# Key tile first, in four pieces, and maxima among the last projections, in a fused attention and FFN kernel

## What is computed

```python
h = layernorm(x)
q  = rms_norm(h @ wq)
k  = rms_norm(ctx @ wk);   ki = rms_norm(ctx @ wki)   # ki for the first 257 rows, k for the rest
v  = ctx @ wv;             vi = ctx @ wvi
x  = x + (attention(q, k, v) + attention(q, ki, vi)) @ wo
t  = layernorm(layernorm(x))[:, -1] @ agg             # one row of each batch
for _ in range(4):
    t = t + gelu(layernorm(t) @ d1) @ d2
y  = layernorm(x)
x  = x + layernorm(y + sigmoid(y @ wg) * (t @ bc))
```

## Time and profile before

| | us |
|---|---|
| runs (three) | 608.13, 610.99, 612.56 |
| median | 610.99 |
| span of the profiled execution | 607.0 |
| PE busy in it | 533.4 (88%) |
| DVE busy | 392.7 (65%) |
| ACT busy | 282.7 (47%) |
| POOL busy | 240.7 (40%) |

### The profile page before, as it was taken

How to read it: one execution, slowest core, us unless ns; L and a number is a source line. 1 busy time by engine, 2 the same in 40 slices (tenths; PEclk the granted TensorE clock), 3 DMA queues, 4 the chain that set the end, 5 groups by cost and what they waited for, 6 DMA issues and landing times.

```text
span 607.0 us, 9796 instructions
## 1 busy us (share of the span) xinstructions
PE 533.4 (88%) x3768; PEld 325.9 (54%) x3768; DVE 392.7 (65%) x750; ACT 282.7 (47%) x504; POOL 240.7 (40%) x138
## 2 busy tenths in 40 slices
PE   2589799999978999989999988898998998999860
PEld 2478668987644555545555454454444544554320
DVE  5547886433965787558776686476565747368676
ACT  3355744552124566426565253536362443376342
POOL 0032330032024766545655533243333345467453
PEclk9988989999979999979999998899999998799976
DMA  7506667599469699927888571707061713100001
GB/s 284 169 1 242 238 248 278 171 209 313 157 165 317 146 214 239 223 88 171 204 214 214 159 170 71 170 10 163 26 146 71 170 37 109 71 1 35 17 37 52
DMA packets 56327, 91.35 MB, mean 150 GB/s; under 512 B 5316, under 2 KB 30276, under 8 KB 55768
## 3 DMA queue, kind: packets, MB, share of 16 engines
q1 hardware_dynamic: 52032, 74.93, 45.8%
q0 software_dynamic: 3184, 14.16, 7.2%
q10 hardware_dynamic: 1064, 1.63, 1.0%
HBM read 70.84 MB, written 19.40 MB: 149 GB/s over the span
## 4 chain that ended last, share of the span: by engine, by line
PE 70%; DVE 16%; ACT 5%; POOL 3%; issue 2%; DMA 2%; SPq 0%; POOLq 0%; ACTq 0%; DVEq 0%
PE psum L673 14%; PE psum L767 12%; PE psum L730 10%; PE psum L748 10%; PE psum L772 5%; PE psum L802 5%; DVE negt L1154 4%; PE psum L891 3%; PE psum L856 3%; PE psum L837 2%; DMA qst<-crow 1%; DVE negm L1152 1%; DVE attT L1170 1%; POOL ssum L1323 1%; POOL ssum L1321 1%
## 5 line engine op out<-in xcount | busy, mean ns | idle before, releaser
L999 ACT ACTIVATE prob<-psum 128x512 f32<-128x512 f32 x256 | 138.6, 593 | 179.9 <-PE psum L748 175.0
L1154 DVE TENSOR_REDUCE negt<-psum 128x1 f32<-128x255 f32 (+1 forms) x256 | 129.2, 545 | 0.0
L1371 POOL TENSOR_TENSOR added<-added,prob 128x1024 f32<-128x1024 f32 x48 | 114.0, 2375 | 24.4 <-ACT prob L999 19.9
L730 PE MATMUL psum<-kst,qst 96*128 96x512 f32 x256 | 100.3, 468 | 5.3 <-DVE negt L1154 5.2
L1368 POOL TENSOR_TENSOR added<-prob 128x1024 f32<-128x1024 f32 x16 | 39.5, 2466 | 158.7 <-ACT prob L999 158.7
L1152 DVE TENSOR_REDUCE negm<-psum 128x1 f32<-128x257 f32 x128 | 53.6, 418 | 74.2 <-PE psum L730 73.6
L748 PE MATMUL psum<-qst,kst 100*128 100x256 f32 x512 | 94.9, 306 | 4.7 <-DMA qst<-crow 3.4
L767 PE MATMUL psum<-prob,vring 128*32 128x256 f32 x1152 | 94.1, 411 | 1.7 <-issue 0.5
L748 PEld LDWEIGHTS psum<-qst,kst 100*128 100x128 f32 x512 | 81.8, 200 | 24.5 <-ACT prob L999 9.6
L730 PEld LDWEIGHTS psum<-kst,qst 96*128 96x128 f32 x256 | 41.4, 195 | 67.5 <-issue 39.6
L1321 POOL TENSOR_TENSOR ssum<-sq 128x512 f32<-128x512 f32 x6 | 9.5, 1585 | 110.7 <-ACT sq L964 110.7
(11 more groups left out here) (150 smaller groups left out, 664.4 us busy)
## 6 DMA issues: line engine op xcount, KB each, us to landing
kst<-kscr SPq DMA_DIRECT2D x96, 256.0 KB, 5.4
vring<-vscr SPq DMA_DIRECT2D x16, 576.0 KB, 8.5
kscr<-hl SPq DMA_DIRECT2D x16, 512.0 KB, 3.0
d<-d POOLq DMA_DIRECT2D x8, 1024.0 KB, 8.3
qst<-qscr SPq DMA_DIRECT2D x96, 64.0 KB, 5.9
vscr<-vbuf SPq DMA_DIRECT2D x18, 256.0 KB, 3.2
raw<-ctxT SPq DMA_DIRECT2D x4, 1024.0 KB, 5.2
qscr<-hl SPq DMA_DIRECT2D x8, 512.0 KB, 3.7
```

The source lines that it names most:

```text
L730: pe.matmul(psum[:, n % 3, :], qst[0:96, slot, jj, qt * P:(qt + 1) * P], kst[0:96, slot, jj, half * 512:(half + 1) * 512], start=True, sto ...
L999: act.activation(prob[:, r % NP, part], score2[:, part], ACT.Exp).then_inc(exp2_done, 1)
L1154: dve.tensor_reduce(negt[:, u % 2, qt, half, j:j + 1], psum[:, n % 3, k0:512], AX.X, ALU.max, negate=True)\
L1371: pool.tensor_tensor(added[:, :], added[:, :], prob[:, r % NP, :], ALU.add).then_inc(added_done, 1)
```

## The change

The order of the plan changes up to the attention, and the loads with it; the attention itself does not. In words:

- The first tile is now the key tile (batch 0, half 1). Its tokens c01 and its weight wk come as four pieces each of 256 KB, by block of the inner dimension: c01 on SP's queue, wk on ACT's, ahead of the three constants. Each piece has its own semaphore and its own split (128x512). The new step `k01(kc)` multiplies block kc for all four quarters into four open banks as soon as its two pieces are split.
- wv, wq and wki are loaded whole and at once into the place of their own low part, and are split there. SP asks for all of it without waiting, together with x, c00 and wvi. Only c00, wvi, c10 and c11 still pass through `raw`.
- Ten small loads (`sel`, `chrow`, `d1b`, `rows`) move from ACT's queue to SP's, behind the inputs.
- After the first tile come v(0, 4..7), then the query tiles, the keys (0, 0), v(0, 0..3), keys (1, 0) and (1, 1), v(1).
- S1(0) to S1(3) stand behind the four quarters of tile 5, S1(4) to S1(11) behind the eight chunks of v(1). The maxima and shift of unit 0 come at chunks 3 and 4 of v(1). Norm(5, 3) is now behind the last chunk and S1(11), directly before `load 2`.
- Each sum of squares has two to five jobs between the last quarter of its tile and itself.
- `load 0` no longer waits for all splits; `load 1` does. ACT's high part of xT(0, .) waits for v(0, 7), and POOL's clearing of `chx` waits for sumsq(5).

```diff
@@ make_plan
+    for kc in range(KC):
+        add('split', 2 * kc)
+        add('split', 2 * kc + 1)
+        add('k01', kc)
+    add('consts')
+    add('split', SPLIT_OF['wv'])
+    proj(0)
     add('xstat', 1)
     add('xnorm', 1)
+    v(0, (4, 5, 6))
+    add('split', SPLIT_OF['wq'])
     for n in range(4):
         add('xT', 1, n)
-    add('split', 0)
-    add('consts')
-    proj(0, (0, 1))
+    v(0, (7,))
+    add('sumsq', 0)
+
+    proj(1, (0,))
     add('xstat', 0)
     add('xnorm', 0)
+    proj(1, (1,))
+    add('norm', 0, 0)
+    proj(1, (2,))
     for n in range(4):
         add('xT', 0, n)
...
+    proj(1, (3,))
+    for oc in range(1, KC):
+        add('norm', 0, oc)
+
+    add('split', SPLIT_OF['c00'])
+    add('split', SPLIT_OF['wki'])
+    proj(2, (0, 1, 2))
+    add('sumsq', 1)
+    proj(2, (3,))
+    add('norm', 1, 0)
+
+    add('split', SPLIT_OF['wvi'])
+    add('norm', 1, 1)
+    proj(3, (0,))
+    add('norm', 1, 2)
+    proj(3, (1,))
+    add('norm', 1, 3)
+    proj(3, (2,))
+    add('sumsq', 2)
+    proj(3, (3,))
+
+    add('norm', 2, 0)
+    v(0, (0,))
+    add('split', SPLIT_OF['c10'])
+    add('norm', 2, 1)
+    v(0, (1,))
+    add('norm', 2, 2)
+    v(0, (2,))
+    add('norm', 2, 3)
+    add('sumsq', 3)
+    v(0, (3,))
+
+    add('norm', 3, 0)
+    add('norm', 3, 1)
+    proj(4, (0,))
+    add('norm', 3, 2)
+    add('split', SPLIT_OF['c11'])
+    proj(4, (1,))
+    add('norm', 3, 3)
     add('load', 0)
+    proj(4, (2, 3))
     add('load', 1)
...
+    for oc in range(KC):
+        proj(5, (oc,))
+        if oc == 2:
+            add('sumsq', 4)
+        add('S1', oc)
     add('load_v', 0)
     add('load_v', 1)
-    v(1, (0,))
-    add('norm', 4, 2)
-
-    for c in range(1, CH):
+    after = {0: (('norm', 4, 0),), 1: (('norm', 4, 1), ('sumsq', 5)), 2: (('norm', 4, 2), ('norm', 4, 3)),
+             3: (('maxes', 0),), 4: (('norm', 5, 0), ('shift', 0)), 5: (('norm', 5, 1),),
+             6: (('norm', 5, 2),), 7: (('norm', 5, 3),)}
+    for c in range(CH):
         v(1, (c,))
-        if c == 1:
-            add('norm', 4, 3)
-            add('sumsq', 5)
-        if c >= 3:
-            add('S1', 2 * c - 6)
-            if 3 <= c < 7:
-                add('norm', 5, c - 3)
-            add('S1', 2 * c - 5)
-            if c == 6:
-                add('maxes', 0)
-    add('shift', 0)
+        add('S1', KC + c)
+        for e in after[c]:
+            add(*e)
     add('load', 2)
     add('phase2')
...
-    for t in range(10, ahead):
-        add('S1', t)
...
-TILES = [('q', 1), ('q', 0), ('k', 0, 0), ('k', 0, 1), ('k', 1, 0), ('k', 1, 1)]
-
-SPLITS = ['wq', 'wki', 'wk', 'c00', 'c01', 'wvi', 'wv', 'c10', 'c11']
+TILES = [('k', 0, 1), ('q', 1), ('q', 0), ('k', 0, 0), ('k', 1, 0), ('k', 1, 1)]
+
+PIECES = [(n, kc) for kc in range(KC) for n in ('c01', 'wk')]
+
+WHOLE = ['wv', 'wq', 'wki']
+
+STAGED = ['c00', 'wvi', 'c10', 'c11']
+
+SPLITS = [n for n, kc in PIECES] + ['wv', 'wq', 'c00', 'wki', 'wvi', 'c10', 'c11']
...
         split_after = {
-            'c00': last_job(lambda e: e[0] == 'proj' and e[1] == 0),
-            'c01': last_job(lambda e: e[0] == 'proj' and e[1] == 1),
-            'wvi': last_job(lambda e: e[0] == 'proj' and e[1] == 1),
-            'c10': last_job(lambda e: e[0] in ('v', 'vimg') and e[1] == 0 and (e[0] == 'vimg' or e[2] < 4)),
-            'c11': last_job(lambda e: e[0] == 'v' and e[1] == 0),
+            'c00': last_job(lambda e: e[0] == 'proj' and e[1] == 1),
+            'wvi': last_job(lambda e: e[0] == 'proj' and e[1] == 2),
+            'c10': last_job(lambda e: e[0] == 'proj' and e[1] == 2),
+            'c11': last_job(lambda e: e[0] in ('v', 'vimg') and e[1] == 0),
         }
@@ SP
+            for kc in range(KC):
+                sp.dma_start(c01_in[:, kc, :], ctx_of('c01')[:, kc, :]).then_inc(piece_loaded[2 * kc], 16)
+            load_whole('wv')
             load_x(1)
-            load_raw(0)
+            load_whole('wq')
             load_x(0)
-            load_raw(1)
+            load_staged(0)
+            load_whole('wki')
+            load_staged(1)
+            sp.dma_start(sel[:, :], T['sel']).then_inc(rows_loaded, 16)
...
             def split(i):
-                if i + 2 < len(SPLITS):
+                if SPLITS[i] in ('c00', 'wvi'):
                     sp.wait_ge(lo_done, i + 1)
-                    load_raw(i + 2)
+                    load_staged(STAGED.index(SPLITS[i]) + 2)
...
                     sp.wait_ge(job_done, job_at[('xT', 0, 3)] + 1)
+                if u == 1:
                     sp.wait_ge(lo_done, len(SPLITS))
@@ PE
+            def k01(kc):
+
+                pe.wait_ge(lo_done, 2 * kc + 2)
+                for oc in range(KC):
+                    job = job_at[('proj', 0, oc, 0)]
+                    for a, b in ((0, 0), (0, 1), (1, 0)):
+                        mm = pe.matmul(psum[:, bank_of[job], :], w_parts['wk'][:, a, kc, oc * P:(oc + 1) * P],
+                                       token_parts[0][:, b, kc, :], start=(kc == 0 and a + b == 0), stop=(kc == KC - 1 and a == 1))
+                    if kc == KC - 1:
+                        mm.then_inc(job_done, 1)
+
@@ ACT
+            for kc in range(KC):
+                act.dma_start(w_in['wk'][:, kc, :], T['wk'][kc * P:(kc + 1) * P, :]).then_inc(piece_loaded[2 * kc + 1], 16)
             for dst, src in ((ident[:, :], T['ident']), (colp[:], T['cols']), (ind_in[:, :], T['ind'])):
                 act.dma_start(dst, src).then_inc(const_loaded, 16)
-
-            def consts():
-                act.wait_ge(const_loaded, 16 * n_const)
-                act.dma_start(sel[:, :], T['sel']).then_inc(rows_loaded, 16)
...
             def split(i):
-                name = SPLITS[i]
-                act.wait_ge(raw_loaded[i % 2], 16 * (i // 2 + 1))
-                if name in split_after:
-                    act.wait_ge(job_done, split_after[name] + 1)
-                dst = w_parts[name] if name[0] == 'w' else token_parts[int(name[2])]
-                act.activation(dst[:, 0], raw[:, i % 2], ACT.Copy).then_inc(hi_done, 1)
+                src, hi, _, loaded, count = split_parts(i)
+                act.wait_ge(loaded, count)
+                if SPLITS[i] in split_after:
+                    act.wait_ge(job_done, split_after[SPLITS[i]] + 1)
+                act.activation(hi, src, ACT.Copy).then_inc(hi_done, 1)
...
+                if h == 0:
+                    act.wait_ge(job_done, job_at[('v', 0, CH - 1)] + 1)
+                act.copy(token_parts[h][:, 0, :, n * P:(n + 1) * P], src).then_inc(xhi_done, 1)
@@ POOL
                     pool.wait_ge(max_done, 24)
+                    pool.wait_ge(job_done, job_at[('sumsq', 5)] + 1)
                     pool.memset(chx[:, :], 0.0).then_inc(chx_zero, 1)
```

More of the change, by code:

```diff
@@ L94, in make_plan @@
     add('xstat', 0)
     add('xnorm', 0)
+    proj(1, (1,))
+    add('norm', 0, 0)
+    proj(1, (2,))
     for n in range(4):
         add('xT', 0, n)
-    proj(0, (2, 3))
-    add('split', 1)
-    add('split', 2)
-    proj(1, (0, 1))
-    add('sumsq', 0)
-    add('split', 3)
-    for tile, before in ((0, None), (1, 4), (2, None)):
-        if before:
-            add('split', before)
-        proj(tile + 1, (2,))
-        add('norm', tile, 0)
-        if tile == 1:
-            add('split', 5)
-        proj(tile + 1, (3,))
-        add('norm', tile, 1)
-        if tile == 1:
-            add('split', 6)
-        if tile < 2:
-            proj(tile + 2, (0,))
-            add('norm', tile, 2)
-            proj(tile + 2, (1,))
-            add('norm', tile, 3)
-            add('sumsq', tile + 1)
-        else:
-            v(0, (0,))
-            add('norm', 2, 2)
-            v(0, (1,))
-            add('norm', 2, 3)
-            add('sumsq', 3)
@@ L128, in make_plan @@
-    for c in range(2, 6):
-        v(0, (c,))
-        if c == 4:
-            add('split', 7)
-        add('norm', 3, c - 2)
-    v(0, (6, 7))
-    add('split', 8)
+    proj(1, (3,))
[12 more added lines that the diff above has]
+    proj(3, (1,))
@@ L431, in build @@
         raw_loaded = [sem(f"raw_loaded{i}") for i in range(2)]
+        piece_loaded = [sem(f"piece_loaded{i}") for i in range(len(PIECES))]
+        whole_loaded = {n: sem("loaded_" + n) for n in WHOLE}
         hi_done = sem("hi_done")
```

90 lines of the change are left out of this document (49 added, 41 removed).

## The result

The changed kernel takes 605.4 us (median of 20 runs, 600.8 to 609.1). The kernel before, run 20 times beside it, takes 609.6 us. The ratio is 0.994, with a 95% interval of 0.992 to 0.996. So the change brings 0.6%, where the prediction says 1.7% (10.6 us). The time lies in the range of the forecast, but the gain is 4.2 us and not 10.6.

| | before | predicted | after |
|---|---|---|---|
| first product of a projection | 19.0 | 7.4 | 8.2 |
| PE ready for S1(0) | | 103.6 | 106.5 |
| S1(0) begins | 149.4 | 110.2 | 115.7 |
| S2(0) begins | 173.7 | 153.9 | 159.3 |
| `load 2` begins | 172.4 | 161.8 | 164.7 |

The account below looks back on a forecast made before the run. The prediction took the time to hang on how much earlier S2(8) starts, set by SP's queue: S2(0) gains 19.8 us, S2(8) only 10.6. So 607.0 - 10.6 = 596.4 us of span, plus 4.0 gives 600.4, range 587 to 606.

Parts of the forecast that it names:

- a wait at S1(16): Step 4 of the attention: PE stalls for pair 4, there at 169.8 us, but this ends well before S2(8).
- every later microsecond then moves with it: Attention behind S2(8): everything later shifts by as much as S2(8) comes earlier, a gain of 10.6 us.
- the 22.5 us from `load 2` to S2(8): SP's queue in unit 0: same bytes and order as before, so S2(8) starts at 161.8 + 22.5 = 184.3 us.
- the wait of 6.5 us for pair 0: Before S1(0): PE ready at 103.6 us waits until pair 0 lands at 110.2; 6.5 us, bounds 0 and 10.
- The first product and PE's work: Start and projections: first product at 7.4 us, then 96.2 us of work, so PE is ready for S1(0) at 103.6.
- T + 10.1: Before `load 0`: norm(3,3) made by T + 7.0 and stored by T + 10.1, with proj(4,0) ending at T = 92.1 us.
- S1(0) to S2(0): Tile 5, v(1) and twelve S1 steps: 43.7 us of PE's work, VectorE keeping up, S2(0) at 153.9 us.
- Norm(5,3) to load 2: Around S2(0): norm(5,3) ends some 4.5 us behind it, its store 3.1 later; `load 2` begins 7.9 us behind S2(0).
- the 4.0 us that were added: Whole kernel: the median of runs, 611.0, lay 4.0 us above the profiled span, so 596.4 became 600.4 us.
- the start does not come early: Rival, start: pieces of `wk` land late, PE starts at 11 to 12 us with gaps; 605 us, chance 0.15.
- the queue does not bind: Rival, unit 0: it takes an undisturbed 17.1 us, S2(8) at 171, gain 23.9; 587 us, chance 0.25.
- VectorE becomes the bound: Rival, v(1): eight norms slowed beside GpSimd's sums end norm(5,3) 21 us later; kernel slower, 621 us, chance 0.05.

Follow-up runs that it names:

- run 20: A count of runs, not a label: the kernel before, without the change, was run 20 times beside the changed kernel: 609.6 us.
- e1_crow_first: Changed kernel with `phase2` (1.5 MB of x, 1 MB of `wo`) issued behind shift(1), so the second `crow` goes first: 595.1 us, ratio 0.979 to the kernel before.
- e3_norm_early: Changed kernel with the four norms of tile 5 one chunk of v(1) earlier each, releasing `load 2` sooner: 603.1 us, ratio 0.993 to the kernel before.
- e4_c11_late: Changed kernel with the split of c11 behind norm(3,3) and `load 0`, not ahead of them: 604.1 us, ratio 0.994 to the kernel before.
- e7_best: New start with a third tail: S1 spread over v(1), `load 1` behind norm(4,1), `load 2` at chunk 6, `phase2` behind shift(1): 593.6 us, ratio 0.977.
- e11_spread: The third-tail kernel with `phase2` in three parts behind shift(1), shift(2), shift(3), and GpSimd's bias eight steps later: 588.1 us, ratio 0.966 to the kernel before.
- e10_split_load: The third-tail kernel with `phase2` in three parts, plus `load 1` in two halves, behind norm(4,1) and norm(4,3): 583.9 us, ratio 0.963.
- e2_old_tail: Changed kernel up to norm(3,3) and `load 0`, with the order of the kernel before behind that: 598.9 us, ratio 0.985 to the kernel before.

## Why the prediction was wrong, and where it was right

It named the right mechanism and the right place: a new wait for pair 0, `load 2` behind S2(0), a wait at S1(16), a wait for `crow`, and SP's queue as what sets S2(8). Experiment e1_crow_first confirms the last. The steps that failed are three prices: that nothing is lost behind S2(8), so that "every later microsecond then moves with it"; that the 22.5 us from `load 2` to S2(8) carry over; and the wait of 6.5 us for pair 0. The span comes out 8.6 us longer than predicted (605.0 against 596.4), and these terms make it up in the profiled execution:

1. **The first product and PE's work, +2.9.** PE is ready for S1(0) at 106.5, not 103.6. The first product is 0.8 late: ScalarE's seven issues ended at 4.90 and not at 4.3. The 48 products of the first tile took 14.0 us, where 10.8 at full rate and 2.1 for the slow clock were reckoned, 1.1 less. The third part is the wait of proj(1,0) for the split of x, 1.9 and not 1.0. The forecast that nothing else opens a gap over 2 us held. Most of this term belongs to the one execution: in e1_crow_first, with the same order up to there, PE is ready for S1(0) at 103.5 and in e3_norm_early at 103.9. That the sum is met so closely there is in part luck, since the late first product and the longer wait were made up by other work that was priced too high.
2. **The wait for pair 0, +2.7.** 9.2 us and not 6.5; in e1_crow_first and e3_norm_early it is 8.9, so this term does not depend on the execution. `load 0` began at 107.7, that is 12.8 us behind T, the end of proj(4,0), at 94.9; the step "T + 10.1" was 2.7 short. The list of VectorE's work in it was incomplete: norm(3,0) to norm(3,2) stand ahead of the subtraction of c11. They keep VectorE from 93.75 us, 0.8 us of it a wait for a store, so the subtraction began at 100.64 (T + 5.7) and not at T + 2.8. Experiment e4_c11_late shows that the split itself is not what one should move: the stores of the norms are next in line.
3. **S1(0) to S2(0), 0.0.** 43.7 us predicted, 43.7 measured. VectorE kept up, so the rival of the slower kernel had no ground.
4. **Norm(5,3) to load 2, -2.5.** It was out 2.6 us behind S2(0) rather than 4.8, with a store of 2.8. `load 2` began 5.4 us behind S2(0), predicted 7.9. (The prediction's own two parts, 4.5 and 3.1, give 7.6.)
5. **load 2 to S2(8), +2.0.** 24.5 us, where the 22.5 of before were carried over. The first tile of x is issued 8.7 us behind the start of `load 2`, before 8.9, so the step lies wholly behind it: from that issue to the landing of `crow` 15.7 us pass (173.45 to 189.15), before 13.6 (181.28 to 194.88). What the plan puts ahead of `crow` is the same, but more bytes moved in the meantime: 4.95 MB in this stretch against 4.50 before, at 315 and 331 GB/s. The 0.45 MB more take 1.4 us at that rate (an estimate), most of the 2.1. They are on SP's queue, and most likely pieces of `load 3`, which SP issued from 182.27, 6.9 us ahead of the landing of `crow`; before it was from 190.62, 4.3 us ahead. The 240 GB/s while PE waits, where 376 stands in the earlier trace rows, fit that: in the kernel before, too, the rate falls when `load 3` follows, to 203 GB/s from 194.9 to 197 us at a DMA share of 0.97. The three other profiles with this order agree in the size: 24.5 to 25.0 us from `load 2` to S2(8). No run holds `load 3` back, so its share is argued and not shown.
6. **"Every later microsecond then moves with it", +5.0.** This is the step that cost most in this execution. The prediction gave unit 1 the 17.1 us of before and looked at nothing behind S2(8). Unit 1 took 22.1 us. Of the difference the half clock behind the 4.4 us wait is about 2.6 us (6.0 us at 0.51), the wait for VectorE's small instruction 1.9, and 0.7 is a gap before S2(16). All three were put at nothing. The wait for `crow` had been foretold; that an idle PE then starts again at 1.2 GHz had been read in the trace of the kernel before and charged twice, for the start and behind the wait for pair 0, but not here. Experiment e1_crow_first removes the wait and with it all three: unit 1 is back at 17.3 us. In the three other profiles that have the wait only the clock's part recurs: unit 1 takes 18.6 to 18.9 us, 1.5 to 1.8 more than reckoned.
7. **The rest, -1.2.** 393.7 us from S2(16) to the end, 394.9 before.

The sum is 2.9 + 2.7 + 0.0 - 2.5 + 2.0 + 5.0 - 1.2 = 8.9, and 0.3 of rounding and of the 17.2 against 17.1 us for unit 1 remain. The step from span to median also failed, to the other side: the 4.0 us that were added are mostly scatter. The profiled execution after is itself a run of 606.8 us with a span of 605.0, so 1.8 us lie around a span, and the kernel before takes 609.6 over 20 runs, where the three runs had 611.0.

Of the rivals, "the start does not come early" did not happen (8.2 us, pieces in time), and "the queue does not bind" did not either, in the changed kernel. It is what e7_best, e11_spread and e10_split_load make true: 16.1 to 16.6 us from S2(0) to S2(8). "VectorE becomes the bound" missed. The thought in it, that a VectorE instruction lasts longer beside GpSimd, was right and decided 1.9 us in this execution, at one instruction of eight columns on PE's path rather than at eight norms.

What the new tail is worth was not asked by the prediction, and should have been. With the new start alone (e2_old_tail) the kernel is faster than with both, by about 5 us, with intervals that touch. The new tail has S1(0) seven jobs earlier in the list, behind proj(5,0) and not behind the fourth chunk of v(1), and so PE reaches it before pair 0 can be there. It also puts norm(5,3), and `load 2` with it, behind the last chunk and S1(11). Neither part was undone by itself; e3_norm_early, which only moves the norms, stays within the noise.

Not settled: how much of the 0.6% each part would carry in an average execution. The profiled executions differ by 3.0 us in two groups of products alone, and those of e3_norm_early and e4_c11_late cannot be told from the changed kernel by time.

## What to carry to other kernels

A queue that is issued in order has a schedule of its own: list the bytes ahead of each small transfer on which the busiest engine waits, and put bulk loads that are needed late behind it, in parts small enough that the next load which is needed soon is not pushed into a wait (here 2.5 MB in one piece cost about 9 us in front of `crow`, and some 6 us behind it, in front of the next load). When a stretch of work is pulled earlier, follow the result past the first point of contact with the old schedule: a wait for `crow` of 4.4 us cost about nine in one execution, since TensorE ran at half clock behind it and then met a slow instruction of VectorE, and in three others waits of 4.9 to 6.3 us cost 1.5 to 1.8 us on top. A profiled execution and the median are a few microseconds apart, so a difference of one percent needs the runs, and the trace only tells where it sits.
